# A causal mask over two PSUM banks in one VectorE instruction, in a transformer block of linear attention and routed experts

## The reference

```python
h = _layernorm(x) * (1 + ca) + sa
q, k, v = jnp.split(h @ w_attn, 3, axis=-1)
q = elu(q) + 1; k = elu(k) + 1                       # per head
S = S + kt[..., :, None] * vt[..., None, :]          # for each token t
z = z + kt
num = einsum('bhi,bhij->bhj', qt, S); den = sum(qt * z)
x = x + ga * ((num / (den + EPS)) @ w_proj)
h = _layernorm(x) * (1 + cb) + sb
one_hot = one_hot(argmax(h @ Wg + bg))
y = gelu(h @ W1[e]) @ W2[e]                          # only the token's expert e counts
x = x + gb * y
```

## Time and profile before

| | us |
|---|---|
| median of 3 runs | 357.5 |
| lowest and highest run | 355.8 and 362.76 |
| span of the profiled execution | 339.4 |
| TensorE matmuls busy | 285.0 (84%) |
| VectorE busy | 241.9 (71%) |
| ScalarE busy | 152.0 (45%) |
| GpSimd busy | 124.8 (37%) |

### The profile page before, as it was taken

The page is one execution under the profiler, slowest core; times in us unless marked ns, Lnnn a source line. Parts: engine busy times, 40 slices in busy tenths (PEclk is TensorE's granted clock), DMA queues, the critical chain, the costliest instruction groups (busy, mean ns, idle before and its releaser), DMA issues.

```text
span 339.4 us, 10754 instructions
## 1 busy us (share of the span) xinstructions
PE 285.0 (84%) x3847; PEld 245.5 (72%) x3847; DVE 241.9 (71%) x842; ACT 152.0 (45%) x301; POOL 124.8 (37%) x142
## 2 busy tenths in 40 slices
PE   1777989999999999999999998942129999999980
PEld 1446678688688788787787887742119999999980
DVE  4974557778778778778687787663735888988880
ACT  3378491780871871861952830000023444444430
POOL 8979000303503404305305205232311546545662
PEclk9997999999999999999999999785558999999995
DMA  7990000001000001001001001000252334333410
GB/s 212 319 302 5 3 2 2 2 3 35 34 4 37 27 0 48 16 0 63 1 0 64 0 0 66 2 34 33 82 162 70 108 90 117 93 95 97 113 38 0
DMA packets 16906, 20.19 MB, mean 59 GB/s; under 512 B 2747, under 2 KB 13117, under 8 KB 16882
## 3 DMA queue, kind: packets, MB, share of 16 engines
q1 hardware_dynamic: 13040, 12.50, 13.1%
q0 software_dynamic: 2832, 6.57, 5.6%
q10 hardware_dynamic: 1010, 0.81, 0.8%
HBM read 12.22 MB, written 8.10 MB: 60 GB/s over the span
## 4 chain that ended last, share of the span: by engine, by line
PE 63%; DVE 15%; issue 6%; ACT 4%; POOL 3%; DMA 3%; DVEq 2%; SPq 1%; POOLq 0%; ACTq 0%
PE bank L1001 18%; PE bank L1013 5%; PE bank L1138 5%; PE bank L1147 4%; PE bank L1033 4%; PE bank L1020 4%; PE bank L956 3%; DVE k_q L885 3%; PE bank L1062 3%; PE bank L979 2%; PE bank L971 2%; ACT h_t L432 2%; POOL sorted_rows L374 2%; PE bank L962 2%; PE bank L1047 2%
## 5 line engine op out<-in xcount | busy, mean ns | idle before, releaser
L374 POOL DMA_INDIRECT sorted_rows<-row_buf,slot_i x32 | 31.6, 987 | 119.7 <-DVE slot_i L777 112.4
L1001 PE MATMUL bank<-q_m,k_q 128*64 128x128 f32 x1024 | 71.9, 284 | 2.6 <-DVE probs L654 2.0
L654 DVE TENSOR_TENSOR probs<-bank,causal 128x256 f32<-128x256 f32 x128 | 51.6, 421 | 22.8 <-PE bank L1001 21.9
L1001 PEld LDWEIGHTS bank<-q_m,k_q 128*64 128x64 f32 x1024 | 56.2, 140 | 10.5 <-DVE probs L654 5.9
L396 POOL DMA_INDIRECT out_dram<-q_m,slot_token x39 | 40.8, 1047 | 44.9 <-DVE q_m L901 27.1
L1138 PE MATMUL bank<-q_m,k_q 128*128 128x128 f32 x312 | 43.0, 283 | 0.0
L1147 PE MATMUL bank<-k_q,v_m 128*128 128x128 f32 x312 | 41.5, 276 | 0.0
L1138 PEld LDWEIGHTS bank<-q_m,k_q 128*128 128x128 f32 x312 | 39.6, 199 | 0.0
L1147 PEld LDWEIGHTS bank<-k_q,v_m 128*128 128x128 f32 x312 | 38.1, 193 | 0.4 <-DVE q_m L898 0.4
L541 ACT ACTIVATE v_m<-bank 128x512 f32<-128x512 f32 x39 | 23.3, 598 | 27.2 <-PE bank L1138 27.2
L484 ACT ACTIVATE rden<-bank 128x512 f32<-128x512 f32 x8 | 4.8, 597 | 49.7 <-PE bank L987 49.6
(11 more groups left out here) (177 smaller groups left out, 510.6 us busy)
## 6 DMA issues: line engine op xcount, KB each, us to landing
v_m<-sorted_rows SPq DMA_DIRECT2D x39, 132.0 KB, 2.1
x_all<-in_L_attn_x_dram SPq DMA_DIRECT2D x16, 128.0 KB, 4.2
w_all<-in_L_ffn_W_dram SPq DMA_DIRECT2D x1, 2048.0 KB, 9.6
out_dram<-q_m,slot_token POOLq DMA_INDIRECT x39, 2.3
sorted_rows<-zeros ACTq DMA_DIRECT2D x4, 132.0 KB, 2.3
sorted_rows<-zeros SPq DMA_DIRECT2D x4, 132.0 KB, 2.5
sorted_rows<-row_buf,slot_i POOLq DMA_INDIRECT x32, 2.4
wmod_sb<-in_L_wmod_dram SPq DMA_DIRECT2D x1, 384.0 KB, 4.8
```

Source lines behind the costliest of these rows:

```text
L374: pool.indirect_dma_start(sorted_rows, bass.IndirectOffsetOnAxis(ap=slot_i[par][:, t:t + 1], axis=0), row_buf[par][:, t, :], None).then_in ...
L654: V.tensor_tensor(probs[:, s, b, q, :], score_bank[q % 2][:, 0:QUADS * L], causal[:].rearrange("p a t -> p (a t)"), ALU.mult).then_inc(pro ...
L1001: last = mm(score_bank[q % 2][L * half:L * half + L, 2 * L * n:2 * L * n + 2 * L], k_q[par][:, q, tok:tok + L], q_m[par][:, 2 * half:2 * h ...
```

## The change

The two banks S0 and S1 become two halves of one PSUM tensor `scores` of 128 x 2 x 512, so that one instruction can read both. `core_probs` issues one multiplication for two quads. It waits until the scores of both are complete, reads 2 x 256 columns, takes `causal` for both halves by a broadcast, and raises `probs_ready` by 2 when it is done. TensorE's code is unchanged, its waits included. The number of masks falls from 128 to 64. The order of all other instructions stays as it is.

```diff
-        bank = [ctx.enter_context(nc.psum_tensor(f"bank{n}", [P, 512], F32)) for n in range(8)]
-        F0, F1, F2, S0, S1, ST, Y0, Y1 = bank
+        F0, F1, F2 = (ctx.enter_context(nc.psum_tensor(f"bank{n}", [P, 512], F32)) for n in range(3))
+        scores = ctx.enter_context(nc.psum_tensor("scores", [P, 2, 512], F32))
+        ST, Y0, Y1 = (ctx.enter_context(nc.psum_tensor(f"bank{n}", [P, 512], F32)) for n in range(5, 8))
+        S0, S1 = scores[:, 0, :], scores[:, 1, :]
...
             def core_probs(g, s, b, quads=range(QUADS)):
                 wait_ge(dve, y_mm, 4 * g + 2 * s - 1)
-                for q in quads:
-                    dve.wait_ge(score_mm, 16 * g + 8 * s + 4 * b + q + 1)
-                    V.tensor_tensor(probs[:, s, b, q, :], score_bank[q % 2][:, 0:QUADS * L],
-                                    causal[:].rearrange("p a t -> p (a t)"), ALU.mult).then_inc(probs_ready, 1)
+                for q in quads[::2]:
+                    dve.wait_ge(score_mm, 16 * g + 8 * s + 4 * b + q + 2)
+                    V.tensor_tensor(probs[:, s, b, q:q + 2, :], scores[:, :, 0:QUADS * L],
+                                    causal[:].rearrange("p a t -> p (a t)").unsqueeze(1).broadcast_to(
+                                        [P, 2, QUADS * L]), ALU.mult).then_inc(probs_ready, 2)
```

## The result

The changed kernel takes 374.2 us, the median of 4 runs between 370.5 and 377.2; the kernel before, run beside it, 359.0 us. The ratio is 1.040, 95% interval 1.030 to 1.050, so by the ratio the change costs 14.2 us (10.7 to 17.7). Predicted were 368.5 us and a loss of 11.0. The range ended at 374.0: the median of the four lies 0.2 us above it, the time by the ratio (357.5 x 1.040 = 371.7 us) inside.

A forecast was written before the change was run, and what follows sets the result against it. TensorE was taken to set the pace, VectorE mattering only where TensorE waits for it. Added stalls of 7.3, 2.9 and 0.8 us, 11.0 in all, gave span 350.4 and time 368.5 us; range 362.0 to 374.0, chance 0.72.

The forecast's parts named there:

- Duration of the mask: Fused 512-column mask on VectorE: 0.69 us, from the residual addition at L685; bounds 434 ns and 0.84 us.
- Rivals 1 (434 ns): VectorE streams a fused mask faster, 434 ns: loss only 4.5 us, time 362.0 us; chance 0.12.
- 2 (0.84): Fused mask costs twice the old, 0.84 us: 3.9 us more, time 372.4 us; chance 0.04.
- The three stalls: Per loop turn: (1,0) FIRST to LAST +0.71, (1,1) FIRST to LAST +0.29, (0,0) LAST to (0,1) FIRST +0.21 us.
- places put at nothing: Behind (0,1) LAST, behind (1,1) LAST, and pairs with a projection or two products between: 0 us added.
- S+1.15: Start of the fused mask, 1.15 us after S, the start of its pair's first scores matmul; formerly S+0.71.
- 7.3 + 2.9 + 0.8 = 11.0 us: Added time: six loop turns 7.3, first group and prologue (with step(0)) 2.9, last group 0.8 us.
- late-VectorE place: Next group's scores (0,0) LAST to (0,1) FIRST, where VectorE is behind: +0.21 us per loop turn.
- 18.1 us lie between it and the median: Profiled span 339.4 against median 357.5 us; the 18.1 us were taken as outside the span and untouched.
- Rival 3, the clock: New idle drops TensorE's granted clock once a turn for about 3 us: 12 us, time 380.5 us; chance 0.07.
- Rival 4, VectorE sets the pace: Shortening VectorE's queue pays: 64 times 154 ns, 9.9 us less, time 347.6 us; chance 0.05.
- Signs: Expected in the profile: masks about 690 ns, turns 25.9 us, TensorE busy time unchanged, loop clock 1.00, VectorE 9 us less.

The follow-up runs named there:

- pair without scatters: Kernel before (two masks) and changed kernel (fused), both with sorting left out and rows written to fixed places by SyncE: 337.2 us and 355.3 us.
- layout run: Kernel before with one PSUM tensor over both banks, its two masks kept: 360.8 us, ratio 1.011.
- pair wait: Kernel before with two masks, but TensorE waits for both masks of the pair before: 361.4 us, ratio 1.013.

## Why the prediction was right, point by point

- **What bounds the kernel.** Right: 1.4 us of added waits on TensorE are 1.41 us on the turn, and a VectorE with 6.9 us less to do (the prediction said 9 or so) gained nothing.
- **Duration of the mask.** 0.69 from the earlier trace rows; measured 0.691. Rivals 1 (434 ns) and 2 (0.84) are out.
- **The three stalls.** All three are there and nearly no other: of the places put at nothing, the one behind (0,1) LAST cost 0.00 where signals came in time, the one behind (1,1) LAST 0.04. Against 0.71, 0.29 and 0.21 they measured 0.77, 0.34 and 0.27. The mis-sized step is the mask's start, S+1.15: it was S+1.21, since an update by two put a semaphore instruction ahead of the mask. With an update by one it was S+1.14 and the turn 25.9 us. A change that only merges instructions altered a form of synchronization too, and that has a price.
- **Sum.** 7.3 + 2.9 + 0.8 = 11.0 us; the pair without scatters gave 8.2 + 3.0 + 1.25 = 12.45. The prediction counted the last group's late-VectorE place (0.27) with the six turns; by its cut that is 8.5, 3.0 and 1.0. The 2.9 was met by terms that were off both ways: up to the first (0,1) FIRST 0.39 instead of 0.70, the next succession 0.78 instead of 0.62, the two of `step(0)` 0.74 each instead of 0.64, the product 0.37 instead of 0.27. On the chip of the result it was 14.2, with 3.5 either way. The 1.8 us left over are within that, and the range's top, 374.0, had no room for them. What the traces have for them is the stretch behind (0,1) LAST, 9.94 us with fused masks and 9.45 in the layout run, 2.4 us over five turns; about 1.6 of that is one clock fall more (three against two).
- **"18.1 us lie between it and the median, and the change touches nothing outside the span."** Wrong, though it didn't spoil the number. Only 1.8 us lie outside a span. The other 16 are late signals and clock falls in the attention loop, in timed executions of before as well (span 358.9). Added to both kernels they nearly cancel here, which is why the difference held, and that is luck: the prediction had no term for them, and with the scatters moved the fused loop turns were some 1.3 us shorter than those of two masks. With two numbers so far apart, the profile was of another kind of execution than the timed ones, and I should have said that rather than put the gap outside.
- **Rival 3, the clock.** The prediction had it at once a turn and 12 us. It fell in three of five loop turns of after, but the unchanged kernel's clock falls in its loop as well (in its second profile at 87.8, 142.4 and 173.1), and where signals come in time the clock of the changed kernel stays at 1.00 in the loop (26.11 us turns), save behind the stop. The idle pieces of 0.86 and 0.28 us at the fused mask had no fall right behind them in any turn of after. The falls of after followed idle pieces of 0.96 to 1.07 and 1.58 to 1.61 us, but 0.98 and 1.64 us in two other turns had none.
- **Rival 4, VectorE sets the pace.** Out: its 347.6 us would have taken shorter turns, and none is under the 24.7 of before.
- **Signs.** "Granted clock 1.00 through the loop", "turns of 25.9" and "busy time of TensorE unchanged" (290.1 against 285.0) failed in the profile of after. On the chip without late signals the clock was 1.00 through the loop's turns, save the one with the stop. The turns were 26.1 us there, and 25.9 with the update by one, whose TensorE was busy 283.9 us.
- The rule of the Trainium skill (Perfetto Trace Analysis, "Matmuls": rotate banks so that emptying one overlaps the next matmuls) agrees with these traces: the 0.44 us of the pair wait and the later start of the mask are that overlap, lost.

## What to carry to other kernels

Two evacuations that alternate between two PSUM banks are a double buffer; one instruction over both makes it a single buffer, and the price is not in the saved instruction but at each place where the next matmuls follow closely: later start plus longer instruction, less what stands between. Count those places before counting instructions, and look at the engine that waits. And set a profile's span against the execution's own time: if timed runs are much longer than the span plus what lies around it (1.8 us here), take another profile before explaining anything by this one.

## What the runs showed of the hardware

- **Late signals of TensorE.** While GpSimd's indirect scatters run, TensorE's semaphores arrived up to 3.5 us behind the modelled ends of the matmuls (0.02 us is usual), on two chips in all eight executions profiled there, and in the profile of after; in two executions with the same scatters on the third chip none was late, and none in the prediction's profile. The lateness moved with the scatters, and the loss was 2.6 us per turn in the layout run and 6.1 where they were moved with two masks, clock falls counted. In that place TensorE's transposes also stood 0.35 to 0.41 us at a time with nothing to wait for in the profile, so a slower TensorE, and not only a late signal, is a rival that wasn't tested. What links them to the scatters is open: reads of TensorE's code are excluded, for 112 to 230 us of after have no packet on queue 8 and every turn in it has late signals. That they depend on the chip is what it looks like with three chips, not more.
- **Code read again inside a loop.** In four of 14 traces (the kernel before once more, two masks with the scatters moved, the changed kernel on the third chip, fused without scatters) TensorE's first scores of a loop round came 3.1 to 4.0 us late while blocks of code were read, with a clock fall behind them; in the last two the turn lost 4.7 and 5.0 us in all. The other traces read no code on that queue between about 113 and 206 us. The Trainium skill, Runtime: NRT & Kernel Launch, section "Instruction fetch mechanics", says that code comes in blocks of 16 KiB and that a taken branch to a block not held stalls; the two packets with 0.03 MB agree with the block size, and place and wait agree with the stall. Why some executions still held the loop's code and others not, no run shows.
- **A semaphore update by two.** The fused mask started 0.07 us earlier with an update by one (S+1.14) than by two (S+1.21). By two each of the 64 masks had a semaphore instruction ahead of it, by one 11 of 64.
